# A graph-network kernel: the ratios of its multi-head attention stage as outer products of key and query rows

## The chip, the cores and the metric

One core of one Trainium2 chip runs the whole kernel. The metric is device time in microseconds of one execution; less is better.

## The reference

64 graphs with 128 nodes of 256 features go through two layers. Layer 0 is softmax attention with 8 heads over masked logits, then a feed-forward block. Layer 1 is graph attention twice: first with 8 heads, then with one. What the change touches is the first of these, for each head:

```python
s = jnp.einsum('bhnk,hk->bhn', h, a_src)
t = jnp.einsum('bhnk,hk->bhn', h, a_dst)
e = jax.nn.leaky_relu(s[:, :, :, None] + t[:, :, None, :], ALPHA)   # ALPHA = 0.2
e = e + bias[:, None, :, :]
attn = jax.nn.softmax(e, axis=-1)
out = jnp.einsum('bhij,bhjk->bhik', attn, h)
```

`bias` is the adjacency matrix, the same for all heads. Since exp(leaky_relu(z)) is the larger of exp(z) and exp(0.2 z), an unnormalised weight is exp(bias) times factors of the row and of the column times max(exp(0.8 (s + t)), 1). The part with max is a rank-one ratio compared with 1.

## The kernel before

The work runs in four stages, A (layer-0 attention), B (feed-forward), C (8-head graph attention) and D (one head). Each goes over the 64 graphs in 16 chunks of four graphs (512 nodes, `W4`). Every engine has its own hand-written instruction list; semaphores join them, and each engine runs strictly in the order that its list gives. Steps 2 to 13 of a stage are a loop of two steps (`chunks`).

Stage C, the subject here, is software-pipelined over two chunks: step i does the front of chunk i and the back of chunk i-1.

The front, in order of data: ScalarE normalises chunk i (`normalise`, `xn`, L944, done at the end of the step before). TensorE transposes it to the PSUM tiles F0 and F1 (`ln_turn`, L1130). ScalarE copies it out as `xh` (L898), VectorE subtracts to get the low part `xl` (`ln_lo`, L293). TensorE then transposes the adjacency into F0 (`adj_turn`, L1184) and computes the score rows s and t of all heads into F1 (`c_st`, L1105 to L1107, six matmuls). VectorE takes row maxima (`rows_max`, `tmx`, L526), ScalarE turns them into shifts (`rows_shift`, `tms`, L1049 and L1050) and exponentiates the rows (`rows_exp`, `rb`, L1056), VectorE caps them (`rows_cap`, L530), TensorE transposes them (`c_b_turn`, L1345), and ScalarE copies them out as rounded rows `rp` (L1024) and columns `bqs` (L1063, with L1064). GpSimd adds the low part of the rows (`rows_lo`, L854). TensorE computes the value rows with `tall` (L1121 to L1123, 24 matmuls in a step), and VectorE scales them into `hb` (`hb_out`, L534).

The back, for each of the 8 heads of chunk i-1: TensorE broadcasts a row of `rp` over all partitions with a selection matmul (`c_bcast`, L1373, 512 columns), VectorE builds the weights `pp` in four instructions of 128 columns, one for each graph, because the column's factor is a scalar of that graph (`c_scale`, L575), and TensorE multiplies by the values in four column tiles (`c_av`, L1385, 16 matmuls in the program, 32 in the trace). The heads alternate between two PSUM banks and two `pp` buffers, so they run one after another:

```python
pe.matmul(BK[:, h % 2, :], sel[:, h, :], rp[par][:], start=True, stop=True).then_inc(c_bc, 1)
...
r = dve.scalar_tensor_tensor(out=pp[h % 2][:, g, :], in0=BK[:, h % 2, g * P:(g + 1) * P],
                             scalar=bq_sb[par][:, g, 16 + h:17 + h], in1=gts(i, g),
                             op0=ALU.max, op1=ALU.mult)
```

At the end ScalarE copies the outputs (`c_out_copy`, `o_sb`, L1083, four copies), VectorE takes reciprocals (`c_recip`, L583) and GpSimd adds the result to x (`residual`, L862 and L868). VectorE also takes the statistics of the next chunk (L276, L281).

## Time and profile before

| | us |
|---|---|
| median of 3 runs (1198.71 to 1200.44) | 1198.84 |
| the profiled execution, its own time | 1199.37 |
| its span in the profile | 1196.3 |
| busy in the span: TensorE, VectorE, ScalarE, GpSimd | 1122.2, 831.5, 704.1, 448.9 |
| busy from 840 to 1035 us (inside stage C) | TensorE 177.38, VectorE 190.25, ScalarE 105.77, GpSimd 147.91 of 195.00 |

Stage C runs from about 814 us (the adjacency transpose of its first chunk) to about 1050 us (its last output copy). Busy time counts an engine from the start of an instruction to its end; successive instructions of an engine overlap a little, so a pitch (start to start) is shorter than a duration. The shares over the whole span mix four stages; the last line of the table is the one that speaks of stage C.

### The profile page before, as it was taken

To read this page: it belongs to the slowest core of one execution; us is meant where nothing else is said; L and a number is where in the kernel's file an instruction comes from. 1 tells how busy PE (TensorE), PEld (TensorE's weight loads), DVE (VectorE), ACT (ScalarE), POOL (GpSimd) and SP (SyncE) were. 2 spreads that over 40 slices of the span, in tenths; PEclk is the share of its full clock that TensorE was granted. 3 is DMA by queue.
4 is the path that set the end of the run, shared out by engine and by line. 5 is a ranking of instruction groups with operands and counts; after the bars stand their busy time and mean duration, and the time that the engine had idled before them with its cause. 6 is when DMAs were issued, how large, how long until landed. Compare 5 with 4: busy or idle time off the path is not lost.

```text
span 1196.3 us, 39899 instructions
## 1 busy us (share of the span) xinstructions
PE 1122.2 (94%) x15260; PEld 966.6 (81%) x15260; DVE 831.5 (70%) x2259; ACT 704.1 (59%) x1734; POOL 448.9 (38%) x657
## 2 busy tenths in 40 slices
PE   5699999999999989999999999998999999869998
PEld 5588888888888769989998998896767667658886
DVE  5676777677777764455445544546999999958886
ACT  2467776777677763355345434543555555559996
POOL 2531212121212112123112311213777777867764
PEclk9799999999999999999999999999999999979999
DMA  8021020111000000000000000000000000002212
GB/s 227 2 73 29 28 55 28 28 29 55 28 12 11 11 2 1 1 1 0 0 0 0 0 0 0 0 1 19 21 18 18 18 18 18 4 1 71 70 53 88
DMA packets 41733, 31.13 MB, mean 26 GB/s; under 512 B 5280, under 2 KB 41376, under 8 KB 41632
## 3 DMA queue, kind: packets, MB, share of 16 engines
q1 hardware_dynamic: 36736, 28.84, 7.8%
q10 hardware_dynamic: 4896, 0.80, 0.6%
q8 instruction: 80, 1.31, 0.4%
q14 instruction: 21, 0.17, 0.1%
HBM read 21.25 MB, written 8.39 MB: 25 GB/s over the span
## 4 chain that ended last, share of the span: by engine, by line
PE 77%; DVE 11%; issue 4%; ACT 4%; POOL 2%; DVEq 1%; DMA 1%; SPq 0%; ACTq 0%; POOLq 0%
PE BK L1229 6%; PE BK L1105 5%; PE BK L1106 5%; PE BK L1107 5%; PE BK L1315 5%; PE BK L1313 5%; PE BK L1314 5%; DVE pp L575 4%; PE BK L1203 4%; PE BK L1215 4%; PE F L1105 3%; PE BK L1196 3%; PE F L1107 3%; PE F L1106 3%; PE F L1130 3%
## 5 line engine op out<-in xcount | busy, mean ns | idle before, releaser
L1005 ACT ACTIVATE gf<-BK,bcol 128x512 f32<-128x512 f32 x128 | 88.3, 690 | 190.6 <-PE BK L1107 176.9
L806 POOL TENSOR_TENSOR ve<-mv,eps_l 128x4 f32<-128x4 f32 x64 | 15.7, 245 | 458.7 <-DVE mv L281 458.7
L924 ACT ACTIVATE e_sb<-BK,nmx 128x128 f32<-128x128 f32 x512 | 141.7, 402 | 28.5 <-DVE nmx L413 28.5
L1313 PE MATMUL BK<-wf_hi,gh 128*128 128x256 f32 x512 | 146.0, 285 | 0.0
L1315 PE MATMUL BK<-wf_lo,gh 128*128 128x256 f32 x512 | 144.8, 283 | 0.0
L1314 PE MATMUL BK<-wf_hi,gl 128*128 128x256 f32 x512 | 143.5, 280 | 0.0
L575 DVE SCALAR_TENSOR_TENSOR pp<-BK,bqs,gt_all 128x128 f32<-128x128 f32 x512 | 137.6, 336 | 3.3 <-PE BK L1385 2.5
L506 DVE TENSOR_TENSOR gl<-gf,gh 128x512 fp32r<-128x512 f32 x128 | 91.7, 716 | 69.1 <-ACT gh L1006 67.0
L419 DVE TENSOR_TENSOR pt_sb<-BK,ft 128x512 f32<-128x512 f32 x128 | 85.1, 686 | 69.2 <-PE BK L1203 67.5
L520 DVE TENSOR_TENSOR x_all<-BK,x_all 128x256 f32 (+1 forms) x64 | 27.2, 425 | 127.4 <-PE BK L1315 127.4
L944 ACT ACTIVATE xn<-x_all,neg_mr,rstd 128x256 f32 (+1 forms) x188 | 100.1, 604 | 24.5 <-POOL neg_mr L815 24.4
L276 DVE BATCH_NORM_STATS2 st<-x_all 128x6 f32 (+1 forms) x256 | 96.8, 413 | 7.7 <-DMA x_all<-in_x_dram 7.6
L1105 PE MATMUL BK<-xh,wf_hi 128*128 128x512 f32 x256 | 101.6, 397 | 0.5 <-DVE x_all L435 0.5
L1106 PE MATMUL BK<-xl,wf_hi 128*128 128x512 f32 x256 | 101.5, 396 | 0.0
L1107 PE MATMUL BK<-xh,wf_lo 128*128 128x512 f32 x256 | 101.4, 396 | 0.0
L1314 PEld LDWEIGHTS BK<-wf_hi,gl 128*128 128x128 f32 x512 | 97.4, 190 | 0.0
L1313 PEld LDWEIGHTS BK<-wf_hi,gh 128*128 128x128 f32 x512 | 96.1, 188 | 0.0
L1315 PEld LDWEIGHTS BK<-wf_lo,gh 128*128 128x128 f32 x512 | 95.8, 187 | 0.0
L783 POOL TENSOR_TENSOR x_all<-x_all,c_bc 128x256 f32 (+1 forms) x128 | 90.0, 737 | 8.6 <-POOL rp L854 8.1
L413 DVE TENSOR_REDUCE nmx<-BK 128x8 f32<-128x1024 f32 x64 | 76.7, 1219 | 23.3 <-PE BK L1196 23.3
L783 POOL TENSOR_TENSOR x_all<-x_all,bo_bc 128x256 f32 (+1 forms) x64 | 44.9, 737 | 125.3 <-ACT xn L944 125.3
L1006 ACT ACTIVATE gh<-BK,bcol 128x512 fp32r<-128x512 f32 x128 | 87.2, 681 | 0.0
(193 smaller groups left out, 2996.8 us busy)
## 6 DMA issues: line engine op xcount, KB each, us to landing
x_all<-in_x_dram SPq DMA_DIRECT2D x16, 512.0 KB, 4.3
adj_in<-in_adj_dram SPq DMA_DIRECT2D x32, 256.0 KB, 2.8
out_dram<-y SPq DMA_DIRECT2D x16, 512.0 KB, 2.9
s_wf<-in_L_gnn_Wf_dram SPq DMA_DIRECT2D x2, 1024.0 KB, 11.8
s_w<-in_L_gnn_W_dram SPq DMA_DIRECT2D x2, 256.0 KB, 7.6
s_wq<-in_L_gnn_Wq_dram SPq DMA_DIRECT2D x1, 256.0 KB, 3.6
s_wk<-in_L_gnn_Wk_dram SPq DMA_DIRECT2D x1, 256.0 KB, 4.1
s_wv<-in_L_gnn_Wv_dram SPq DMA_DIRECT2D x1, 256.0 KB, 4.9
```

The costliest lines, as they stand in the source:

```text
L276: dve.bn_stats(st[:, g, :], xs(i, g)).then_inc(ln_st, 1)
L506: dve.tensor_tensor(gl[:, f, :], gf[f % 2][:], gh[:, f, :].bitcast(F32), ALU.subtract).then_inc(b_gl, 1)
L575: r = dve.scalar_tensor_tensor(out=pp[h % 2][:, g, :], in0=BK[:, h % 2, g * P:(g + 1) * P], scalar=bq_sb[par][:, g, 16 + h:17 + h], in1=gt ...
L783: pool.tensor_tensor(xs(i, g), xs(i, g), bias[:], ALU.add).then_inc(signal, 1)
L924: e = act.activation(e_sb[:, j, :], LE[:, r, q, :], ACT.Exp, bias=nmx[:, j:j + 1], scale=1.0)
L944: act.activation(xn[:, g, :], xs(nxt, g), ACT.Identity, scale=rstd[:, g:g + 1], bias=neg_mr[:, g:g + 1]).then_inc(ln_xn, 1)
L1105: pe.matmul(dst, w_hi, m_hi, start=start, stop=False)
L1106: pe.matmul(dst, w_hi, m_lo, start=False, stop=False)
L1107: return pe.matmul(dst, w_lo, m_hi, start=False, stop=stop)
L1313: pe.matmul(dst, gh[:, f, n], hi[:, f, :], start=(f == 0), stop=False)
L1314: pe.matmul(dst, gl[:, f, n], hi[:, f, :], start=False, stop=False)
L1315: r = pe.matmul(dst, gh[:, f, n], lo[:, f, :], start=False, stop=(f == FT - 1))
```

## The change

In stage C alone, the row broadcast goes. The score rows of four heads now lie in four groups of 32 partitions, key rows and query rows in one tile. VectorE takes minima (`row_minima`), ScalarE moves them to the other half of the partitions (`far_minima`, two tiny activations), VectorE combines them (`row_shifts`), ScalarE exponentiates (`row_exps`: four activations with a scale and a bias that are both columns in memory), VectorE caps (`row_limits`). ScalarE then makes two tiles `inv` with the halves exchanged (`inverse_rows`, two activations of 64 partitions x 512 columns for each group of four heads). `ratios` computes exp(0.8 (s + t)) as outer products: 16 matmuls for four heads, in four row tiles of the array, into four banks. VectorE needs no column factor any more, the constant 1 takes its place, so `c_scale` is one instruction of 512 columns for a head. Two banks are left for outputs; heads are collected in groups of 3, 3 and 2, each copied out by one activation. There are four `pp` buffers and two `o_sb` buffers. `rows_lo` and the copy to `rp` leave stage C. Stage D keeps its own path with a smaller `sel`. The setup computes masks and scales for the new layout, in place of the wide `sel`: 17 more small VectorE instructions (11 for masks by partition, 5 more for the weights of the rows, 1 for their bias).

The order within a step is rewritten on all engines. The core of the diff:

```diff
+HEAD_GROUPS = ((0, 3), (3, 3), (6, 2))
...
-        sel = sb("sel", [P, H, P], F32R)
+        sel = sb("sel", [P, P], F32R)
...
+        o_sb = [o(f"o_sb{r}", [P, G, H * HA]) for r in range(2)]
-        pp = [o(f"pp{r}", [P, G, P]) for r in range(2)]
-        o_sb = o("o_sb", [P, G, H * HA])
+        pp = [o(f"pp{r}", [P, G, P]) for r in range(4)]
+        row_e = o("row_e", [P, W4])
+        row_c = o("row_c", [P, W4])
+        inv = [o(f"inv{r}", [P, W4]) for r in range(2)]
...
-                done(dve.tensor_tensor(sel[:], ident[:, 0:H].unsqueeze(2).to_broadcast([P, H, P]),
-                                       ident[:, 32:32 + H].unsqueeze(2).to_broadcast([P, H, P]), ALU.add))
+                done(dve.tensor_tensor(sel[:], ident[:, 0:1].to_broadcast([P, P]), ident[:, 32:33].to_broadcast([P, P]), ALU.add))
...
+            def row_minima(i):
+                dve.wait_ge(c_st_done, i + 1)
+                dve.tensor_reduce(row_mn[:], ROW[CC][:].rearrange("p (g n) -> p g n", n=P), AX, ALU.min).then_inc(r_mn, 1)
+            def row_shifts(i):
+                dve.wait_ge(r_far, i + 1)
+                dve.wait_ge(r_mn, i + 1)
+                dve.scalar_tensor_tensor(out=row_sh[:], in0=row_mn[:], scalar=own_row[:, 0:1], in1=far_mx[:],
+                                         op0=ALU.mult, op1=ALU.add).then_inc(r_sh, 1)
+            def row_limits(i):
+                dve.wait_ge(r_e, i + 1)
+                wait_for(dve, r_q, i * 2)
+                dve.tensor_scalar(row_c[:], row_e[:], row_cap[:, 0:1], None, ALU.min).then_inc(r_c, 1)
             def hb_out(e, par, n):
...
-            def c_scale(i, par, h):
-                dve.wait_ge(c_bc, i * H + h + 1)
+            def c_scale(i, h):
+                dve.wait_ge(r_q, i * 2 + h // 4 + 1)
                 dve.wait_ge(c_gt, i + 1)
-                wait_for(dve, c_o, i * H + (h - 1))
-                for g in range(G):
-                    r = dve.scalar_tensor_tensor(out=pp[h % 2][:, g, :], in0=BK[:, h % 2, g * P:(g + 1) * P],
-                                                 scalar=bq_sb[par][:, g, 16 + h:17 + h], in1=gts(i, g),
-                                                 op0=ALU.max, op1=ALU.mult)
-                r.then_inc(c_pp, 1)
...
             def c1_step(i, half, par):
                 back = not (isinstance(i, int) and i == 0)
-                for h in range(H):
-                    if back:
-                        c_scale(i - 1, 1 - par, h)
-                    c1_front(i, par, h)
-                    if h == 1 and back and not (isinstance(i, int) and i == 1):
-                        c_recip(i - 2)
+                if back:
+                    c_scale(i - 1, 0)
+                if back and not (isinstance(i, int) and i == 1):
+                    c_recip(i - 2, par)
+                if back:
+                    c_scale(i - 1, 1)
+                    ln_lo(i + CC)
+                    c_scale(i - 1, 2)
+                    c_scale(i - 1, 3)
+                row_minima(i)
+                next_stats(i, (0, 1))
+                row_shifts(i)
+                next_stats(i, (2, 3))
+                dve.wait_ge(ln_st, (i + CC + 2) * G)
+                if back:
+                    c_scale(i - 1, 4)
+                aggr(i + CC + 1)
+                row_limits(i)
+                if back:
+                    c_scale(i - 1, 5)
+                    c_scale(i - 1, 6)
+                    c_scale(i - 1, 7)
+                dve.wait_ge(c_bq, i + 1)
+                hb_out(i, par, 0)
+                hb_out(i, par, 1)
...
+                        add_bias(i, CC, c1_bc, c_xb)
+                        if not (isinstance(i, int) and i < 2):
+                            residual_share(i - 2, par)
-                        rows_lo(i, par)
-                        add_bias(i, CC, c1_bc, c_xb)
+                    if first == CC and not (isinstance(i, int) and i < 2):
+                        residual_sum(i - 2)
...
+            def c1_step(i, half, par):
+                back = not (isinstance(i, int) and i == 0)
+                if back and not (isinstance(i, int) and i == 1):
+                    c_out_copy(i - 2, par, 2)
+                if back:
+                    ln_hi(i + CC)
+                act.wait_ge(adj_t, i + NC + 1)
+                act.activation(gt_all[:, bass.ds(i * W4, W4)], F[0][:], ACT.Exp).then_inc(c_gt, 1)
+                if back:
+                    c_out_copy(i - 1, 1 - par, 0)
+                far_minima(i)
+                row_exps(i)
+                inverse_rows(i, 0)
+                bq_out(i, par, 0)
+                if back:
+                    c_out_copy(i - 1, 1 - par, 1)
+                normalise(i, CC, range(G))
+                inverse_rows(i, 1)
+            def far_minima(i):
+                act.wait_ge(r_mn, i + 1)
+                wait_for(act, r_sh, i)
+                for to, of in ((0, 64), (64, 0)):
+                    r = act.activation(far_mx[to:to + 64, :], row_mn[of:of + 64, :], ACT.Identity, bias=cb[0][of:of + 64, 0:1],
+                                       scale=far_row[of:of + 64, 0:1])
+                r.then_inc(r_far, 1)
+            def row_exps(i):
+                act.wait_ge(r_sh, i + 1)
+                wait_for(act, r_c, i)
+                for g in range(G):
+                    r = act.activation(row_e[:, g * P:(g + 1) * P], ROW[CC][:, g * P:(g + 1) * P], ACT.Exp, bias=row_sh[:, g:g + 1],
+                                       scale=row_sign[:, 0:1])
+                r.then_inc(r_e, 1)
+            def inverse_rows(i, t):
+                act.wait_ge(r_c, i + 1)
+                for to, of in ((0, 64), (64, 0)):
+                    r = act.activation(inv[t][to:to + 64, :], row_c[of:of + 64, :], ACT.Copy, scale=half_row[of:of + 64, t:t + 1])
+                r.then_inc(r_inv, 1)
...
+            def c_out_copy(i, par, k):
+                first, heads = HEAD_GROUPS[k]
+                if k == 0:
+                    wait_for(act, c_att, (i - 1) * G + C_START)
+                act.wait_ge(c_o, i * H + first + heads)
+                act.activation(o_sb[par][:, :, first * HA:(first + heads) * HA],
+                               BK[:, 4 + (par + k) % 2, 0:G * heads * HA].rearrange("p (g c) -> p g c", g=G), ACT.Copy).then_inc(c_ev, 1)
...
-            def c_bcast(i, par, h):
-                pe.wait_ge(c_rp, i + 1)
-                pe.wait_ge(c_lo, i + 1)
-                wait_for(pe, c_pp, i * H + (h - 1))
-                pe.matmul(BK[:, h % 2, :], sel[:, h, :], rp[par][:], start=True, stop=True).then_inc(c_bc, 1)
+            def ratios(i, t):
+                pe.wait_ge(r_inv, i * 2 + t + 1)
+                pe.wait_ge(c_one, i + 1)
+                wait_for(pe, c_pp, i * H + 4 * t)
+                for g in range(G):
+                    n = slice(g * P, (g + 1) * P)
+                    for r in range(4):
+                        rows = slice(r * 32, r * 32 + 4)
+                        m = pe.matmul(BK[:, r, n], inv[t][rows, n], row_c[rows, n], start=True, stop=True, tile_position=(r * 32, 0))
+                m.then_inc(r_q, 1)
...
+            def c_h_out(g):
+                r = tall(F[g // 2][:, (g % 2) * D:(g % 2 + 1) * D], "w1", g, g % 2 == 0)
+                if g % 2 == 1:
+                    r.then_inc(c_h, 1)
             def c1_step(i, half, par):
                 back = not (isinstance(i, int) and i == 0)
-                for h in range(H):
-                    if back and h < H - 1:
-                        c_bcast(i - 1, 1 - par, h + 1)
-                    c1_front(i, half, par, h)
-                    if h == H - 2:
-                        c_bcast(i, par, 0)
-                    if back:
-                        c_av(i - 1, 1 - par, h)
+                if back:
+                    ratios(i - 1, 0)
+                c_turn(i, CC)
+                if back:
+                    c_av(i - 1, 1 - par, 0)
+                adj_turn(i + CC, half, par, CC)
+                if back:
+                    c_av(i - 1, 1 - par, 1)
+                c_st(i, CC, 0)
+                c_st(i, CC, 1)
+                if back:
+                    c_av(i - 1, 1 - par, 2)
+                    c_av(i - 1, 1 - par, 3)
+                    ratios(i - 1, 1)
+                pe.wait_ge(c_gt, i + 1)
+                c_h_out(0)
+                c_h_out(1)
+                if back:
+                    c_av(i - 1, 1 - par, 4)
+                row_turn(i)
+                pe.wait_ge(r_e, i + 1)
+                c_h_out(2)
+                c_h_out(3)
+                if back:
+                    c_av(i - 1, 1 - par, 5)
+                    c_av(i - 1, 1 - par, 6)
+                    c_av(i - 1, 1 - par, 7)
...
```

What the order looks like on TensorE around the transpose of the exponentiated rows, in a loop step of before (`rb` are the rows, `sel` the broadcast, `hb,pp` a head's output):

```order
L1385 MATMUL BK<-hb_95,pp_103 32x33 [waits c_pp]
L1385 MATMUL BK<-hb_95,pp_103 32x33 x15
L1373 MATMUL BK<-rp_99,sel 128x512 [waits c_pp,c_lo,c_rp]
L1345 MATMUL F<-ident,rb 128x128 [waits c_rb]
L1345 MATMUL F<-ident,rb 128x128 x3
L1376 REGISTER_ALU
L1385 MATMUL BK<-hb_95,pp_104 32x33 [waits c_pp]
```

and in a loop step of the change (`row_c` are the capped rows; L1212 is the first of the 12 value matmuls of two graphs, L1470 a head's output):

```order
L1470 MATMUL BK<-hb_100,pp_108 32x33 [waits c_pp]
L1470 MATMUL BK<-hb_100,pp_108 32x33 x15
L55 ISA [waits r_c]
L1437 MATMUL BK<-ident,row_c 128x128 [waits c_pp]
L1437 MATMUL BK<-ident,row_c 128x128 x3
L1212 MATMUL F<-w_hi,xh 128x256 [waits r_e]
```

Before, outputs of three heads still follow the transpose one by one with their broadcasts between them. In the change, 12 value matmuls stand behind the transpose, and the outputs of heads 5, 6 and 7 stand behind those.

On ScalarE, in a loop step of the change, from the exponentials to the end of the step (`o_sb` is the copy of heads 3 to 5 of the chunk before, `xn` the normalisation of the next chunk):

```order
L1105 ACTIVATE row_e<-F,row_sh,row_sign 128x128 [waits r_c,r_sh]
L1105 ACTIVATE row_e<-F,row_sh,row_sign 128x128 x3
L1112 ACTIVATE inv_117<-row_c,half_row 64x512 [waits r_c]
L1112 ACTIVATE inv_117<-row_c,half_row 64x512
L1152 ACTIVATE bqs_101<-BK 128x4x8 [waits r_t]
L1155 ACTIVATE hb_99<-BK 128x32
L1174 REGISTER_ALU
L1175 ACTIVATE o_sb_98<-BK 128x4x99 [waits c_o]
L1003 ISA [waits ln_nm]
L1005 ISA [waits ln_t]
L1005 ACTIVATE xn<-x_all,neg_mr,rstd 128x256
```

Before, the normalisation follows directly on the two small copies of the transposed rows, and all output copies stand at the start of a step. Now a copy that waits for head 5 stands ahead of the normalisation.

## Rows read from the trace of the kernel before

**Rows 1.** Windows: us, busy PE, PEld, DVE, ACT, POOL, granted clock, DMA share, GB/s

```profile
840.00:1035.00 195.00, 177.38 (x4189) 136.54 (x4187) 190.25 (x641) 105.77 (x271) 147.91 (x230) 1.00 0.06 17
...
822.00:825.00 3.00, 3.00 (x14) 2.35 (x14) 0.97 (x3) 1.48 (x4) 2.92 (x5) 0.51 0.00 0
...
1045.00:1050.00 5.00, 3.03 (x131) 1.79 (x131) 3.61 (x14) 0.74 (x3) 1.54 (x3) 1.00 0.02 3
```

**Rows 2.** Groups by line of VectorE, 840 to 1035: xcount | busy us, mean ns | idle

```profile
L575 DVE SCALAR_TENSOR_TENSOR pp<-BK,bqs,gt_all 128x128 f32<-128x128 f32 x433 | 116.4, 335 | 3.0 <-PE BK L1385 2.5
L293 DVE TENSOR_TENSOR xl<-F,xh 128x512 fp32r<-128x512 f32 x28 | 17.9, 681 | 0.0
...
L530 DVE TENSOR_SCALAR rb<-rb 40x512 f32<-40x512 f32 x14 | 10.3, 738 | 0.0
L526 DVE TENSOR_REDUCE tmx<-F 24x4 f32<-24x512 f32 x14 | 9.7, 692 | 1.7
...
L583 DVE RECIPROCAL crec<-o_sb 128x32 f32<-128x32 f32 x14 | 4.7, 335 | 0.0
```

**Rows 3.** Timeline of ScalarE, 900 to 930: start us, us, [idle before]

```profile
903.15 0.39 ACT L1049 ACTIVATE tms<-tmx,cb,msc 24x4 f32<-24x4 f32 x1 [2.52 <-DVE tmx L526]
...
917.51 0.39 ACT L1049 ACTIVATE tms<-tmx,cb,msc 24x4 f32<-24x4 f32 x1 [2.52 <-DVE tmx L526]
...
918.39 1.12 ACT L1056 ACTIVATE rb<-F,tms 40x128 f32<-40x128 f32 x4
...
922.56 2.08 ACT L944 ACTIVATE xn<-x_all,neg_mr,rstd 128x256 f32 x4 [0.32 <-POOL neg_mr L815]
925.29 1.24 ACT L1083 ACTIVATE o_sb<-BK 128x264 f32<-128x264 f32 x4 [0.65 <-PE BK L1385]
```

**Rows 4.** Groups by line, whole span: VectorE and ScalarE forms near the new ones

```profile
L419 DVE TENSOR_TENSOR pt_sb<-BK,ft 128x512 f32<-128x512 f32 x128 | 85.1, 686 | 69.2 <-PE BK L1203 67.5
...
L1072 ACT ACTIVATE hb<-BK,bqs 128x256 f32<-128x256 f32 x64 | 26.9, 472 | 5.7 <-PE BK L1123 4.2 <-issue 0.3
...
L930 ACT ACTIVATE att_t<-BK 128x256 f32<-128x256 f32 x64 | 25.5, 399 | 36.8 <-PE BK L1222 36.8
...
L1024 ACT ACTIVATE rp<-rb 40x512 fp32r<-40x512 f32 x16 | 10.1, 632 | 17.0 <-DVE rb L530 17.0
...
L354 DVE TENSOR_TENSOR sel<-ident 128x1024 fp32r<-128x1024 f32 x1 | 1.2, 1207 | 0.0
```

**Rows 5.** Timeline of TensorE in stage C: start us, us

```profile
814.41 0.48 PE L1105 MATMUL F<-xh,wst_hi 128*128 128x512 f32 x1
...
815.66 0.40 PE L1107 MATMUL F<-xh,wst_lo 128*128 128x512 f32 x1
...
913.60 0.66 PE L1184 MATMUL F<-ident,adj_in 128*128 128x128 f32 x4 [0.33 <-DVE xl L293]
...
916.61 0.46 PE L1385 MATMUL BK<-hb,pp 128*32 128x33 f32 x32
917.00 0.50 PE L1373 MATMUL BK<-rp,sel 128*128 128x512 f32 x1
917.33 0.28 PE L1121 MATMUL F<-w_hi,xh 128*128 128x256 f32 x1
...
921.23 0.60 PE L1345 MATMUL F<-ident,rb 128*128 128x128 f32 x4
...
922.49 0.28 PE L1121 MATMUL F<-w_hi,xh 128*128 128x256 f32 x1
...
924.04 0.49 PE L1373 MATMUL BK<-rp,sel 128*128 128x512 f32 x1
```

**Rows 6.** Timeline of TensorE in stage A: 16 f32 matmuls in four row tiles

```profile
301.50 1.17 PE L1196 MATMUL BK<-k,q 32*128 32x128 f32 x32
302.60 0.76 PE L1215 MATMUL BK<-v,pt_sb 128*32 128x33 f32 x64
```

**Rows 7.** Tile rb in stage D: duration ns min/median/max, first and last start

```profile
L530 DVE TENSOR_SCALAR rb<-rb x15: 410/419/707, 1059.9 to 1177.7; 40x512 f32<-40x512 f32 x15
```

More of the change, by code:

```diff
@@ L43 @@
 ROWS = 40
+HEAD_GROUPS = ((0, 3), (3, 3), (6, 2))
+FACTOR_SHIFT = 40.0
+RATIO_LIMIT = 5.5e34
+FACTOR_LIMIT = 6.4e17
 TROW = 96
@@ new lines, in inverse_rows, with c2_front @@
+            def inverse_rows(i, t):
[3 more added lines that the diff above has]
+                r.then_inc(r_inv, 1)
+            def c2_front(i, par):
+                if not (isinstance(i, int) and i == 0):
+                    d_hb(i - 1, 1 - par, 1)
+                normalise(i, CD, range(G))
+                rows_shift(i)
+                wait_for(act, c_lo, i)
+                rows_exp(i)
+                if not (isinstance(i, int) and i == NC - 1):
+                    d_hi(i + 1, 1 - par)
+                wait_for(act, d_bc, i - 1)
+                act.wait_ge(c_rb, i + 1)
+                act.activation(rp[par][0:ROWS, :], rb[0:ROWS, :], ACT.Copy).then_inc(c_rp, 1)
+                bq_out(i, par, 1)
@@ L1077, in _ @@
             act.wait_ge(c_zero, 6)
-            def c_out_copy(i):
-                wait_for(act, c_att, i * G + C_START)
-                for g in range(G):
-                    act.wait_ge(c_o, (i + 1) * H)
-                    act.activation(o_sb[:, g, :], BK[:, 2 + g, 0:H * HA], ACT.Copy).then_inc(c_ev, 1)
-            def c1_step(i, half, par):
-                if not (isinstance(i, int) and i < 2):
-                    c_out_copy(i - 2)
-                c_front(i, par, CC)
+            def c_out_copy(i, par, k):
[5 more added lines that the diff above has]
+                               BK[:, 4 + (par + k) % 2, 0:G * heads * HA].rearrange("p (g c) -> p g c", g=G), ACT.Copy).then_inc(c_ev, 1)
             chunks(act, c1_step)
-            c_out_copy(NC - 2)
+            last = (NC - 1) % 2
+            c_out_copy(NC - 2, 1 - last, 2)
             d_hi(0, 0)
-            c_out_copy(NC - 1)
+            for k in range(len(HEAD_GROUPS)):
+                c_out_copy(NC - 1, last, k)
             def c2_step(i, half, par):
-                c_front(i, par, CD)
+                c2_front(i, par)
                 d_hb(i, par, 0)
@@ L1375, in c_av @@
             def c_av(i, par, h):
+                k = h // 3
+                first, heads = HEAD_GROUPS[k]
                 pe.wait_ge(c_pp, i * H + h + 1)
@@ L1403, in _ @@
             last = (NC - 1) % 2
-            for h in range(H):
-                if h < H - 1:
-                    c_bcast(NC - 1, last, h + 1)
-                c_av(NC - 1, last, h)
+            for t in range(2):
+                ratios(NC - 1, t)
+                for h in range(4 * t, 4 * t + 4):
+                    c_av(NC - 1, last, h)
             def d_bcast(i, par):
-                pe.wait_ge(c_rp, i + NC + 1)
-                pe.wait_ge(c_lo, i + NC + 1)
+                pe.wait_ge(c_rp, i + 1)
+                pe.wait_ge(c_lo, i + 1)
                 wait_for(pe, d_pp, i * G)
-                pe.matmul(BK[:, 0, :], sel[:, 0, :], rp[par][:], start=True, stop=True).then_inc(d_bc, 1)
+                pe.matmul(BK[:, 0, :], sel[:], rp[par][:], start=True, stop=True).then_inc(d_bc, 1)
             def d_av(i, par, g):
```

223 lines of the change are left out of this document (107 added, 116 removed).

## The prediction

> **What bounds the kernel now.** The change touches stage C and a little of the setup, so I read the windows first, and of them the one that lies inside stage C [rows 1]. VectorE is busy 190.25 of 195.00 us there, 97.6%, against 91% of TensorE, 54% of ScalarE and 76% of GpSimd. The timeline of ScalarE gives the length of a step: the same shift instruction starts at 903.15 and at 917.51 [rows 3], 14.36 us a chunk. The groups of VectorE [rows 2] say what fills it: L575, the weights, takes 116.4 us; 433 instructions are 13.5 chunks of 32, so 8.6 us of each 14.36. The rest of VectorE's work is 14.0 - 8.6 = 5.4 us a chunk. So VectorE's throughput bounds stage C, and more than half of it is what the change rewrites.
>
> TensorE's timeline [rows 5] gives pitches (start to start). A head's output takes 0.39 (916.61 to 917.00), a broadcast 0.34 (917.00 to 917.33), 12 value matmuls 1.55 (922.49 to 924.04), four transposes at most 0.60, the six score matmuls 1.25 from first to last start. In a chunk: 8 x 0.39 + 8 x 0.34 + 24 value matmuls 3.1 + 1.5 for the scores + 16 transposes 2.2 = 12.6 us.
>
> **The change, throughput first.** VectorE: 32 instructions of 128 columns become 8 of 512. The nearest row reads PSUM and memory over 512 columns in 0.686 [rows 4]; successive ones overlap by about 0.08, so 0.60 each, 4.8 instead of 8.6. Maxima to minima is the same instruction; the cap goes from 40 to 128 partitions at 512 columns, same length. The new `row_shifts` has 4 columns: under the 0.335 of the 32-column reciprocal [rows 2] and over nothing, I take 0.17. VectorE would need 10.4 us.
> TensorE: 8 broadcasts (2.7) go, two groups of 16 f32 matmuls in four row tiles come. Stage A has this form with 32 rows a tile instead of 4: 1.10 from start to the next start [rows 6]. The columns that stream are the same, so 2.2: 12.1 us.
> ScalarE: 7.8 us a chunk now; minus the copy to `rp` (0.63), plus four inverse copies (below) 2.5, plus 0.4 for the exponentials: 10.1. GpSimd loses `rows_lo`.
> No engine is above 12.1 us. If throughput decided, a chunk would fall by some 2 us. It doesn't say what the waits do, so I followed the chain that returns to itself after one step.
>
> **The loop of waits in the new order.** It starts where normalisation starts on ScalarE.
> 1. Four `xn`: 2.08 less an overlap of 0.10, 1.98 [rows 3].
> 2. Behind them in the queue, the second pair of inverse copies. A copy of 512 columns from memory takes 0.632, and a scale that is a column in memory adds 0.07 (472 ns for 256 columns against 399) [rows 4]: 0.70 each, 1.20 to the next start.
> 3. The last output copy (264 columns) 0.40, the reciprocal on VectorE that waits for it 0.26 to the next start, then `pp` of head 1, 0.60. Only now comes `ln_lo`: 0.68 for its first half [rows 2]. The transposes and `xh` are ready earlier.
> 4. TensorE: adjacency 0.60, head 1 0.39, scores 1.65 (814.41 to the end of the last, 815.66 + 0.40) [rows 5].
> 5. Minima 0.69 [rows 2]; two small activations, 0.39 each [rows 3], 0.79; `row_shifts` 0.17.
> 6. Four exponentials. Before, with a bias column, four took 1.12 [rows 3], 0.356 the last and 0.255 apart. Now the scale is a column too. I add 0.1 to each: 1.54. Lower end 1.12; upper end the four `xn` with both columns, 2.08.
> 7. The cap. 0.738 in stage C, 0.419 in stage D [rows 2, 7]. In stage C GpSimd was adding tensors at that moment; in the new order its only work then is the tiny `ve`. I take 0.42, and 0.74 is the upper end.
> 8. TensorE: transposes of the rows 0.55, 12 value matmuls 1.51, head 5 0.46 [rows 5]. These follow strictly, although head 5 needs neither.
> 9. ScalarE: the copy of heads 3 to 5, 0.40 to the next start, which stands ahead of the normalisation in the queue: back at 1.
>
> The sum is 14.29. Nine hand-overs between engines lie in it; from the shifts' end to the exponentials' start there are 0.09 us (917.51 + 2 x 0.39 to 918.39) [rows 3], I take 0.06 each, 0.55. The loop branch, once in two steps, and register work between waits: 0.15. So 15.0 us a step, against 14.36 now. TensorE stands idle almost 3 us of it: about 1.7 for `ln_lo` (its first half is done 3.1 after the `xn` end: 1.20 + 0.40 + 0.26 + 0.60 + 0.68 less 0.10, with hand-overs; eight transposes and head 0 fill 1.4), the rest before the transposes of `xn` and of the rows. The freed 3.8 us of VectorE are waits, hidden behind the loop.
>
> The ScalarE steps are where a rule of the skill can be weighed. Four exponentials with one column operand took 1.12 us [rows 3]. The Trainium skill, "ScalarE: Activation LUTs", section "What ACT_TABLE_LOAD costs", puts an activation at 186 ns plus 0.833 ns an element plus about 93 ns for each pointer operand, with about 93 ns of overlap. By that the old four would take 1.27, so it is high for a PSUM source, and the new four 1.64; the sum would be 15.1 instead of 15.0.
>
> **Sum.** 14 steps run at full length with both halves: 14 x 0.64 = +9.0 us. Draining the last chunk: before 8 heads at 4 x 0.27 (116.4 / 433) behind a broadcast, about 9.0; after, two `ratios` with hand-over at 1.2, 8 x 0.60 and an output, 7.5: -1.5. Setup, on VectorE's list before stage A is in swing: `sel` (1.207) [rows 4] shrinks to an eighth, -1.0; 17 small instructions come, each under 0.335 [rows 2]; at 0.12, +2.0; net +1.0, with 0 and +3 as ends. Total +8.5. The profiled execution took 1199.37, 0.53 over the median: 1207.9, and **1207** against the median of 1198.84.
>
> **Rivals.**
> *Throughput decides (faster).* The loop falls apart if one long link is not in it: above all if head 5 ends before the normalisation's inputs are ready, or if `ln_lo` doesn't wait for the last output copy. Then a step is TensorE's 12.1 plus about 1 us of waits, 13.1: 14 x -1.26 = -17.6, with drain and setup -18, 1180. The point is where the loop passes under 14.36: 0.64 shorter than I sum it. Low exponentials (-0.42) and inverse copies at 0.6 (-0.2) bring it only just there. For it speaks that VectorE has 4 us to spare; against it, that both waits stand ahead of their followers in a strict queue. 0.15.
> *Nothing gained.* The low ends of 6 and 2 together: 14.4, and 1199. 0.13.
> *Slower than the sum: the TensorE clock.* TensorE would be idle 3 of 15 us, now 1.3. In rows 1 the granted clock is 0.51 from 822 to 825, at 1.2 GHz, after TensorE had been mostly waiting for the first chunk's rows; it is 1.00, 2.4 GHz, from 1045 to 1050 with 3.03 of 5 us busy. If the clock fell in the 1.7 us gap, scores, adjacency and outputs behind it would double: about +2 us a step, 17.0, 1236. The second row has TensorE idler than the new order would, so 0.06. The Trainium skill, "TensorE: Matmul & The Clock Gate", Part 1, says that the gate follows how busy the engine has been, which would give 1236 by the same working; by that rule alone I would give it more.
> *The change doesn't do what it says:* row tiles that run one after another would make `ratios` 4.4 us; 2 x 3.3 less TensorE's slack beside them (1.2) is 5.4 a step, 1283; rows 6 show the form at 1.10. Under 0.01.
> My own case, the loop at 14.7 to 15.4 (exponentials 0.3 shorter, or the cap at 0.74), holds 0.65: 1202 to 1217.
>
> **How the numbers follow.** About 0.2% (2.4 us) is what a measurement of this kernel can tell from no change. Faster 0.15 is the first rival, same 0.13 the second, slower 0.72 my case with the clock and the fourth. The range reaches from 1188, which takes in half of the throughput case, to 1220, with the upper ends of the links; outside are about 0.08 below and 0.10 above.
>
> **What would show it.** In the profile after: `pp` with 128x512, x128, near 0.68 us each; VectorE busy in stage C down from 97.6% to about 70%, ScalarE up to about 68%; a step of 15.0 us from one `far_mx` to the next; `ratios` 1.1 us from start to the next start; a wait of ScalarE at `o_sb` for TensorE's output in each step of about 1 us, and TensorE waiting more than 1 us for `xl` before the adjacency. I am wrong if a step is under 14.4 us, if ScalarE's normalisation waits for GpSimd's `neg_mr` instead of following `o_sb`, or if stage C, 236 us from 814 to 1050 now, doesn't become 7 to 10 us longer.

## The result, and the profile after

The changed kernel takes 1227.3 us (median of 4 runs, 1226.1 to 1227.97) against 1198.9 before (1198.71 to 1200.44): the ratio is 1.0232, interval 1.0219 to 1.0245. It is slower, as forecast, but by 28 us instead of 8, and above the range. The profiled execution took 1226.1 us with a span of 1224.3.

The page of the changed kernel: span, busy time of TensorE and VectorE, the granted clock in 40 slices, and the group of scaling copies (busy us, mean ns | idle before).

```profile
span 1224.3 us, 41293 instructions
...
PE 1127.3 (92%) x16156; PEld 984.7 (80%) x16156; DVE 781.3 (64%) x1908; ACT 743.7 (61%) x1766; POOL 426.7 (35%) x641
...
PEclk9799999999999999999999999998778877779999
...
L614 DVE SCALAR_TENSOR_TENSOR pp<-BK,gt_all 128x512 f32<-128x512 f32 x128 | 82.5, 678 | 34.3 <-PE BK L1454 31.8
```

The copies are what was foreseen, 8 a chunk of 0.678 us where there were 32 of 0.335 us [rows 2], and VectorE has 50 us less to do (781.3 against 831.5). But nine slices of the clock row, from 826 us to 1102, nearly all of stage C and the first of stage D, stand at 7 and 8. The windows of the changed kernel (columns as in [rows 1]: us, busy PE, PEld, DVE, ACT, POOL, granted clock), first most of stage C, then one step of it in pieces of 2 us:

```profile
860.00:1030.00 170.00, 145.09 (x3657) 120.57 (x3656) 106.58 (x240) 103.21 (x220) 95.83 (x160) 0.80 0.05 15
...
888.00:890.00 2.00, 1.88 (x16) 1.84 (x16) 1.96 (x4) 1.77 (x4) 1.50 (x5) 1.00 0.00 0
890.00:892.00 2.00, 1.57 (x110) 1.38 (x112) 1.12 (x2) 1.38 (x3) 2.00 (x3) 1.00 0.00 0
892.00:894.00 2.00, 1.65 (x34) 1.46 (x30) 0.69 (x1) 1.96 (x5) 1.48 (x4) 0.85 0.00 0
894.00:896.00 2.00, 1.49 (x37) 1.01 (x35) 0.89 (x3) 1.93 (x4) 2.00 (x4) 0.50 0.00 0
896.00:898.00 2.00, 1.34 (x24) 1.01 (x28) 2.00 (x5) 0.09 (x1) 2.00 (x5) 0.50 0.00 0
898.00:900.00 2.00, 2.00 (x32) 1.65 (x24) 0.40 (x1) 0.51 (x1) 0.37 (x1) 0.50 0.29 86
900.00:902.00 2.00, 2.00 (x83) 1.50 (x86) 1.12 (x3) 0.66 (x2) 0.00 (x0) 0.94 0.15 45
```

The granted clock that was 1.00 from 840 to 1035 us [rows 1] is now 0.80 on average: once in every step it falls from 2.4 to 1.2 GHz and comes back. With two levels, a mean of 0.80 means that it is at half for 0.4 of each step, 6.8 of 17.04 us. VectorE is busy 63% (106.58 of 170). What the half clock does is in the timeline of the changed kernel, one step (start us, duration us):

```profile
884.80 0.78 ACT L1097 ACTIVATE far_mx<-row_mn,cb,far_row 64x4 f32<-64x4 f32 x2
...
890.62 0.51 ACT L1175 ACTIVATE o_sb<-BK 128x396 f32<-128x396 f32 x1 [0.79 <-PE BK L1470]
891.02 2.06 ACT L1005 ACTIVATE xn<-x_all,neg_mr,rstd 128x256 f32 x4
...
893.14 1.75 PE L1221 MATMUL F<-ident,xn 128*128 128x128 f32 x8 [0.35 <-ACT xn L1005]
894.58 0.39 ACT L1175 ACTIVATE o_sb<-BK 128x264 f32<-128x264 f32 x1
...
896.66 1.12 PE L1275 MATMUL F<-ident,adj_in 128*128 128x128 f32 x4 [1.18 <-DVE xl L312]
...
897.71 0.67 PE L1470 MATMUL BK<-hb,pp 128*32 128x33 f32 x32
...
898.31 0.80 PE L1196 MATMUL F<-xh,wst_hi 128*128 128x512 f32 x1
...
900.88 0.69 DVE L581 TENSOR_REDUCE row_mn<-F 128x4 f32<-128x512 f32 x1 [2.48 <-PE F L1198]
...
901.84 0.38 ACT L1097 ACTIVATE far_mx<-row_mn,cb,far_row 64x4 f32<-64x4 f32 x1
```

A step is 17.04 us (884.80 to 901.84), against 14.36 [rows 3]. The waits of the changed kernel in 825 to 1050 (us in total, times, longest) are those that the loop was built from: ScalarE's output copies for TensorE, and TensorE for `xl`.

```profile
ACT o_sb L1175 <- PE BK L1470: 47.1, 26, 3.1
...
DVE crec L620 <- ACT o_sb L1175: 23.3, 14, 2.0
...
PE F L1275 <- DVE xl L312: 15.6, 13, 2.0
```

Something else moved that the change doesn't touch. Stage B, whose code is the same, runs from 444.9 to 797.8 us instead of 447.4 to 813.2: 352.9 us long instead of 365.8. The tile view of its matmuls (ns min/median/max, first and last start), before:

```profile
L1313 PE MATMUL BK<-wf_hi,gh x512: 279/286/365, 447.4 to 813.0; 128*128 128x256 f32 x171
...
L1315 PE MATMUL BK<-wf_lo,gh x512: 276/281/285, 447.8 to 813.2; 128*128 128x256 f32 x171
```

and after:

```profile
L1404 PE MATMUL BK<-wf_hi,gh x512: 276/276/369, 444.9 to 797.6; 128*128 128x256 f32 x171
...
L1406 PE MATMUL BK<-wf_lo,gh x512: 276/276/281, 445.3 to 797.8; 128*128 128x256 f32 x171
```

So the 28.0 us between the spans are: -2.5 up to stage B, -12.9 in it, +39.5 in the 15 steps of stage C (first to last row minima 253.6 us; before, first to last shift 214.1), and +3.9 between stage B and these steps and behind them.

### The profile page after: what moved, and what is told of

It is laid out like the page before. It is cut to its first block, busy times and chain, and to the rows that moved or that the text cites. A ratio compares the mean times of both kernels' runs of the same rounds, so it can differ in the third digit from the quotient of the medians.

```text
span 1224.3 us, 41293 instructions
## 1 busy us (share of the span) xinstructions
PE 1127.3 (92%) x16156; PEld 984.7 (80%) x16156; DVE 781.3 (64%) x1908; ACT 743.7 (61%) x1766; POOL 426.7 (35%) x641
## 4 chain that ended last, share of the span: by engine, by line
PE 71%; ACT 9%; DVE 8%; issue 6%; POOL 3%; ACTq 1%; DVEq 1%; DMA 0%; POOLq 0%
PE BK L1320 5%; PE BK L1198 5%; PE BK L1197 5%; PE BK L1196 5%; PE BK L1404 5%; PE BK L1405 5%; PE BK L1406 5%; PE BK L1294 4%; PE F L1196 4%; PE BK L1306 4%; PE F L1221 3%; PE F L1197 3%; PE F L1198 3%; PE BK L1287 3%; ACT xn L1005 2%
## 5 line engine op out<-in xcount | busy, mean ns | idle before, releaser
L862 POOL TENSOR_TENSOR ve<-mv,eps_l 128x4 f32<-128x4 f32 x64 | 15.1, 236 | 533.0 <-DVE mv L300 533.0
L1404 PE MATMUL BK<-wf_hi,gh 128*128 128x256 f32 x512 | 142.9, 279 | 0.0
L1406 PE MATMUL BK<-wf_lo,gh 128*128 128x256 f32 x512 | 141.5, 276 | 0.0
L614 DVE SCALAR_TENSOR_TENSOR pp<-BK,gt_all 128x512 f32<-128x512 f32 x128 | 82.5, 678 | 34.3 <-PE BK L1454 31.8
L1221 PE MATMUL F<-ident,xn 128*128 128x128 f32 x512 | 78.4, 304 | 13.9 <-ACT xn L1005 13.6
```

The costliest lines, as they stand in the source:

```text
L1221: r = pe.transpose(F[kt][:, g * P:(g + 1) * P], xn[:, g, kt * P:(kt + 1) * P], ident[:])
L1404: pe.matmul(dst, gh[:, f, n], hi[:, f, :], start=(f == 0), stop=False)
L1406: r = pe.matmul(dst, gh[:, f, n], lo[:, f, :], start=False, stop=(f == FT - 1))
```

## The experiments

There were two questions: where stage C lost 39 us, and why stage B is shorter. For the first my theory was the loop of waits with the falling clock on top of it; the rivals were that the loop is longer than summed, whatever the clock, or that TensorE is bound by its own work. For the second the theory was the place of tiles in memory: `sel` shrinks by 3584 bytes a partition and small tiles are new, so that the tiles behind them move by 3424 bytes. Among them is what stage B multiplies: `gh` starts at byte 163904 of a partition instead of 167328, and `xh` and `xl` at the same place as `gh` modulo 256. The weights lie ahead of `sel` and don't move. The rival was something carried over from stage A.

### Stage B: tiles moved, nothing else

The kernel before with an unused tile ahead of those that moved:

```diff
         exp_bias = sb("exp_bias", [P, 1])
+        sb("pad", [P, 8])
```

> The kernel before with 32 bytes of unused memory ahead of the activation tiles, so that xh, xl, gh and gl start at a multiple of 64 bytes, as they do in the changed kernel (before: 32 over a multiple of 64). Theory (the start address sets the pitch of stage B's matmuls, 0.120 us against 0.116 for 256 columns): stage B 13 us shorter, stage C unchanged at 236.6, about 1186 us. Rival (stage B got faster for another reason, such as the code's place or the run): 1199 us, pitch 0.120.

Measured: 1192.89 us (1191.27 to 1193.68), ratio 0.9949 (0.9933 to 0.9966). Stage B took 446.4 to 806.3, 359.9 us. The place counts, but half of the effect was missing. The same pad in the changed kernel:

> The changed kernel with the same 32 bytes, which puts its activation tiles 32 over a multiple of 64. Theory of the start address: stage B takes 366 us again, 1240 us. Rival: no change, 1227 us.

Measured: 1239.73 us (1237.26 to 1240.03), stage B 363.3 us (447.3 to 810.6). Moving 32 bytes takes the gain away again, so it belongs neither to the changed code nor to stage A. Larger pads in the kernel before (`[P, 168]`, `[P, 40]` and `[P, 104]`) ask which distance counts:

> The kernel before with an unused tile of 672 bytes a partition ahead of the tiles of stage B, so that they start at the same place within 4096 bytes as in the changed kernel (32 bytes gave 1192.9 us, stage B 360 us long instead of 366; the changed kernel's is 353). If the start within a larger stride than 64 bytes decides, stage B is about 353 us and the time about 1186 us. If only the start within 64 bytes counts, it is 1193 us as with 32 bytes, and the other 7 us of the changed kernel's stage B come from the order of the tiles among themselves.

> The kernel before with an unused tile of 160 bytes a partition: the tiles of stage B then start at the same place within 512 bytes as with 672 bytes (1184.0 us), but not within 1024, 2048 or 4096. If the place within 512 bytes or less decides, stage B is 353 us long and the time about 1184 us; if a larger stride counts, it stays between that and the 1192.9 us that 32 bytes gave, or above.

> The kernel before with an unused tile of 416 bytes a partition: the tiles of stage B start at the same place within 256 bytes as with 160 and 672 bytes (1183.3 and 1184.0 us), but 256 bytes off within 512. If the place within 256 bytes or less decides, stage B is 353 us long again and the time 1182 to 1185 us; if it is the place within 512, stage B is longer and the time above 1187 us.

Measured: 1183.97 us (1182.44 to 1185.85), 1183.32 (1182.1 to 1184.34) and 1183.47 (1182.1 to 1184.44), the last with ratio 0.9868 (0.9852 to 0.9885). The tile view of the kernel before with 416 bytes:

```profile
L1314 PE MATMUL BK<-wf_hi,gh x512: 276/276/369, 445.9 to 797.9; 128*128 128x256 f32 x171
...
L1316 PE MATMUL BK<-wf_lo,gh x512: 276/276/278, 446.2 to 798.2; 128*128 128x256 f32 x171
```

By the start byte of `gh`:

| kernel | start mod 256 | mod 512 | stage B, us |
|---|---|---|---|
| before | 160 | 416 | 365.8 |
| changed, 32 bytes on | 96 | 96 | 363.3 |
| before, 32 bytes on | 192 | 448 | 359.9 |
| before, 672 bytes on | 64 | 64 | 352.9 |
| before, 160 bytes on | 64 | 64 | 352.8 |
| before, 416 bytes on | 64 | 320 | 352.3 |
| changed | 64 | 64 | 352.9 |

The four with 64 agree within 0.6 us, whatever the place within 512. So stage B's -12.9 us is a gift of memory placement. Part of the -2.5 us ahead of stage B is too: with the pads of 160, 416 and 672 bytes stage B begins at 445.5, 445.9 and 445.8 us instead of 447.4. The fair partner of the changed kernel is the moved kernel before with 1184.0 us, and against it the change costs 43 us, not 28. Which of the moved tiles makes the difference, and through what, was not tried.

### Stage C: work that nobody reads

The clock fell where TensorE had waits in every step. If the fall is part of the price, filling a wait buys it back:

```diff
+                if back:
+                    for n in range(7):
+                        pe.matmul(BK[:, 4 + (1 - par) % 2, 396:512], ident[:], ident[:, 0:116], start=True, stop=True)
                 adj_turn(i + CC, half, par, CC)
```

> The changed kernel with seven f32 matmuls of 116 columns into unused columns of a bank, in each step between the output of head 0 and the adjacency transposes, where TensorE waits for xl. They fill about 1.35 us of the wait at full clock. Theory (of the 17.05 us of a step, 15.0 are the loop of waits and 2.0 the fallen clock): the clock stays at 1.0, a step takes 15.0 to 15.3, total about 1199 us. Rival (the loop alone is 17 us long, and the clock only falls because TensorE waits): the step stays at 17 or grows by up to 1.4, 1227 to 1248 us.

Measured: 1212.62 us (1209.8 to 1215.71), 14.7 us under the changed kernel, with 7 matmuls a step more. The timeline of this kernel, one step in which the clock stayed at 1.00 (L1489 are the filler matmuls; each stands in the trace as two):

```profile
880.73 1.50 ACT L1105 ACTIVATE row_e<-F,row_sh,row_sign 128x128 f32<-128x128 f32 x4 [0.29 <-DVE row_sh L586]
...
882.37 0.48 DVE L592 TENSOR_SCALAR row_c<-row_e,row_cap 128x512 f32<-128x512 f32 x1
...
882.98 0.65 PE L1437 MATMUL BK<-ident,row_c 128*128 128x128 f32 x4 [0.30 <-DVE row_c L592]
883.39 0.37 PE L1212 MATMUL F<-w_hi,xh 128*128 128x256 f32 x1
...
884.94 1.06 PE L1470 MATMUL BK<-hb,pp 128*32 128x33 f32 x96
885.48 0.51 ACT L1175 ACTIVATE o_sb<-BK 128x396 f32<-128x396 f32 x1 [0.79 <-PE BK L1470]
885.88 2.06 ACT L1005 ACTIVATE xn<-x_all,neg_mr,rstd 128x256 f32 x4
...
887.96 1.45 ACT L1112 ACTIVATE inv<-row_c,half_row 64x512 f32<-64x512 f32 x2
...
889.40 1.82 PE L1489 MATMUL BK<-ident 128*128 128x116 f32 x14
889.44 0.39 ACT L1175 ACTIVATE o_sb<-BK 128x264 f32<-128x264 f32 x1
...
891.51 0.66 PE L1275 MATMUL F<-ident,adj_in 128*128 128x128 f32 x4 [0.29 <-DVE xl L312]
...
892.49 0.50 PE L1196 MATMUL F<-xh,wst_hi 128*128 128x512 f32 x1
...
894.18 0.69 DVE L581 TENSOR_REDUCE row_mn<-F 128x4 f32<-128x512 f32 x1 [0.93 <-PE F L1198]
...
895.14 0.78 ACT L1097 ACTIVATE far_mx<-row_mn,cb,far_row 64x4 f32<-64x4 f32 x2
...
896.21 1.50 ACT L1105 ACTIVATE row_e<-F,row_sh,row_sign 128x128 f32<-128x128 f32 x4 [0.29 <-DVE row_sh L586]
```

It separates the two causes, because this step and that of the changed kernel are the same up to the adjacency transposes: from `far_mx` to there 11.86 us in both (884.80 to 896.66; 879.65 to 891.51). Behind them the half clock adds, to the head 0.46 (1.05 against 0.59), to the scores 0.21 (0.60 against 0.39), to the minima 0.88 (2.57 against 1.69), together 1.55. The loop by itself is 15.48 us (880.73 to 896.21), and with the clock 17.04. The transposes of `xn`, 1.75 instead of 1.09, cost nothing: `xl` is waited for anyway.

In five of its 15 steps the clock still fell (16.5 to 16.7 us each, where the others from the third step on took 15.5 to 15.7), so the fill was a partial cure. That is some 5 us of the 13.6 over the 1199 expected; 7 more are the loop, 15.5 instead of 15.0. In such a step the fillers themselves ran at half clock:

```profile
905.09 3.34 PE L1489 MATMUL BK<-ident 128*128 128x116 f32 x14
...
908.22 0.66 PE L1275 MATMUL F<-ident,adj_in 128*128 128x128 f32 x4
```

They took 3.34 us instead of 1.82, more than the gap holds, and pushed the adjacency transposes back: no wait for `xl` is left ahead of them. Four of these matmuls instead of seven:

> The changed kernel with four instead of seven matmuls of 116 columns that nobody reads ahead of the adjacency transposes: about 1.05 us of work in a gap of about 2.1 us (with seven it was 1.82 us, and 0.3 us of the gap was left). A step in which the clock held took 15.49 us there, one in which it fell 17.05. If what decides is that TensorE isn't left idle in this gap, four hold the clock in fewer steps than seven: between 1213 and 1227 us. If any work in the gap is enough, the time is that with seven or less, 1206 to 1213 us.

Measured: 1206.23 us (1205.08 to 1207.94). The time is that of the second theory, but it isn't a proof of it, because the clock did not hold more often. In the profiled executions it fell in 7 of 15 steps with four fillers (0.95 in 860 to 1030 us) and in 5 of 15 with seven (0.97). What is less is the price of a fall: 15.8 to 16.3 us for such a step instead of 16.5 to 16.7. Four fillers just about fit into the gap even at half clock:

```profile
904.36 2.04 PE L1489 MATMUL BK<-ident 128*128 128x116 f32 x8
```

Less fill was faster, then, not better at holding the clock. The steps account for 2.4 of the 4.9 us between the two profiled executions; 1.0 was there before stage B began, and the rest lies behind the steps and isn't explained. One execution of each is profiled, so that 7 and 5 may be chance. That 1206 is so near the forecast's 1207 is luck: the 15 steps are 19.8 us longer than before where 9.0 was forecast, and the placement, which the forecast didn't have, takes 12.9 off.

### Stage C: one link out of the loop

ScalarE's copy of heads 3 to 5 stood ahead of the normalisation. Behind it:

```diff
-                if back:
-                    c_out_copy(i - 1, 1 - par, 1)
                 normalise(i, CC, range(G))
+                if back:
+                    c_out_copy(i - 1, 1 - par, 1)
                 inverse_rows(i, 1)
```

> The changed kernel with ScalarE's copy of heads 3 to 5 behind the normalisation instead of ahead of it. Theory of the loop: the wait for head 5 leaves the loop, and the step is 0.8 us shorter at whatever clock: 14.4 with the clock full (1190 us), 16.2 with the clock falling once a step (1214 us); I expect the second. Rival (the copy was not on the path): no change, 1227 us.

Measured: 1220.64 us (1219.03 to 1222.96), 6.7 us less than the changed kernel where 13 was expected. From its fourth step to its 14th a step took 17.0 to 17.2 us as in the changed kernel; the first three and the last were shorter, together by 3.4 us. The timeline of TensorE in this kernel says why:

```profile
895.00 1.11 PE L1275 MATMUL F<-ident,adj_in 128*128 128x128 f32 x4 [1.52 <-DVE xl L312]
...
896.64 0.80 PE L1196 MATMUL F<-xh,wst_hi 128*128 128x512 f32 x1
...
898.94 0.63 PE L1198 MATMUL F<-xh,wst_lo 128*128 128x512 f32 x1
899.50 1.11 PE L1470 MATMUL BK<-hb,pp 128*32 128x33 f32 x64
900.54 1.38 PE L1454 MATMUL BK<-row_c,inv 4*128 4x128 f32 x32
```

All six scores, and the outputs and ratios behind them, now run at half clock; in the changed kernel the last scores and what follows are fast again (900.77 0.78). The fall begins later behind the row minima (11.5 us against 9.5) and covers more of what the loop waits for: the clock took back what the link gave. With four filler matmuls as well:

> Four of these matmuls, and ScalarE's copy of heads 3 to 5 behind the normalisation. If the normalisation is what the step waits for, it starts 0.8 us or more sooner, and the time is 11 us or more under that with the four matmuls alone. If the chain beside it (ratios of the last two heads, their scaling copy, their value matmuls, the last output copy) ends at the same time, as the copy alone let one think with 6.6 us of gain, it is 3 to 7 us under it.

Measured: 1193.84 us (1191.92 to 1197.95), 12.4 under the four matmuls alone, ratio 0.9962 (0.9947 to 0.9977). With the clock mostly held (0.99 in 860 to 1030) the same edit is worth twice as much, and the mean step is 14.84 instead of 15.59. Not all of it is the link: from the third on, steps at full clock went from 15.5 to 15.6 down to 14.9 to 15.1, and the clock fell in 2 steps instead of 7. The copy was a link of the loop, as summed, and edits on such a loop can only be priced together with the clock.

### Stage C: the links out of the loop

The reciprocal moves on VectorE, the last output copy, the second pair of inverse copies and the copy of heads 3 to 5 on ScalarE:

```diff
                     c_scale(i - 1, 0)
-                if back and not (isinstance(i, int) and i == 1):
-                    c_recip(i - 2, par)
...
                 row_minima(i)
+                if back and not (isinstance(i, int) and i == 1):
+                    c_recip(i - 2, par)
...
-                if back and not (isinstance(i, int) and i == 1):
-                    c_out_copy(i - 2, par, 2)
                 if back:
                     ln_hi(i + CC)
+                if back and not (isinstance(i, int) and i == 1):
+                    c_out_copy(i - 2, par, 2)
...
                 if back:
+                    inverse_rows(i - 1, 1)
                     c_out_copy(i - 1, 1 - par, 0)
...
+                normalise(i, CC, range(G))
                 if back:
                     c_out_copy(i - 1, 1 - par, 1)
-                normalise(i, CC, range(G))
-                inverse_rows(i, 1)
...
+            inverse_rows(NC - 1, 1)
```

> The changed kernel with its links taken out of the loop: on ScalarE the copies of the last output and of heads 3 to 5 and the inverse copies are issued behind what the next step waits for, and on VectorE the reciprocal of the last group goes behind the row minima. No arithmetic is changed. Loop of waits with the clock on top (my theory): the step is then near VectorE's and TensorE's own work, about 13.2 us where the changed kernel takes 17.05, TensorE's granted clock stays above 0.97 in 860 to 1030 us, and the time is 1227 - 14 x 3.9 = about 1173 us (1165 to 1185). Rival, TensorE is bound by its own work at whatever clock it gets: the clock stays near 0.80 and the time above 1215 us. Rival, another wait of the same size takes the place of each: 1195 to 1215 us.

Measured: 1178.71 us (1178.56 to 1181.83), ratio 0.9834 (0.9815 to 0.9853). It beats the changed kernel by 48.6 us and the kernel before by 20. Of those 20 some 15 are the placement of stage B: against the moved kernel before (1183.97, run on the same chip) the gain is 5.3 us, and the two sets of runs do not overlap. A step takes 13.89 us on average (first to last row minima, 801.93 to 1010.27, 15 steps), more than the 13.2 that I expected. The window of this kernel:

```profile
860.00:1030.00 170.00, 147.62 (x4498) 124.97 (x4498) 128.49 (x283) 122.91 (x259) 116.08 (x192) 0.97 0.05 15
```

TensorE is busy 147.62 of 170, 12.06 us a step, at a clock of 0.97; VectorE 10.5. One step in which the clock fell took 15.68, the others 12.5 to 14.25. So the "throughput" numbers of the forecast, 12.1 and 10.4, were right, and about 1.8 us of waits remain, where the rival "throughput decides" had 1. The same with the narrow copies:

```diff
-                dve.scalar_tensor_tensor(out=pp[h % 4][:].rearrange("p g n -> p (g n)"), in0=BK[:, h % 4, :], scalar=1.0,
-                                         in1=gt_all[:, bass.ds(i * W4, W4)], op0=ALU.max, op1=ALU.mult).then_inc(c_pp, 1)
+                for g in range(G):
+                    r = dve.scalar_tensor_tensor(out=pp[h % 4][:, g, :], in0=BK[:, h % 4, g * P:(g + 1) * P], scalar=1.0,
+                                                 in1=gts(i, g), op0=ALU.max, op1=ALU.mult)
+                r.then_inc(c_pp, 1)
```

> As the kernel with the links cut, but with each 512-column scaling copy on VectorE done as four of 128 columns, as before the change (the constant 1 stays). It prices the wide copies where VectorE bounds: 8 copies of 0.68 us against 32 of about 0.22 is +1.6 us a step if VectorE bounds, so 14.8 us a step and about 1195 us. If TensorE or a loop of waits bounds instead, the difference is under 0.5 us a step and the time within 7 us of the other.

Measured: 1197.03 us (1194.0 to 1201.65), as the first theory said, but by another way. Its windows:

```profile
860.00:1030.00 170.00, 144.57 (x4136) 121.47 (x4136) 138.75 (x537) 117.54 (x250) 108.50 (x180) 0.96 0.06 16
```

VectorE is busy 82%, not bound. Undisturbed steps take 14.4 us, 0.2 to 0.6 more than with wide copies; but in six of the 15 the clock falls and they take 16.2 to 16.3 (it falls in the first step too, which takes 14.1). So of the 18.3 us some 11 (6 x 1.8) are again the clock. And four filler matmuls on the kernel with the links cut:

> As the kernel with the links cut, with four matmuls of 116 columns that nobody reads ahead of the four adjacency transposes, where TensorE was idle. If the clock still falls with the links cut, this gives back what it costs and the time is under that kernel's by 5 us or more; if it stays up already, the filler is hidden in idle time or costs at most 4 x 0.1 us a step, 0 to +6 us.

Measured: 1184.66 us (1183.72 to 1190.47), 6.0 more: 4 x 0.1 us in each of 15 steps. The clock fell in one step, as without them. Where the clock holds, filler is plain cost.

## Why the prediction was wrong

The lengths of a step, worked out from the starts of the row minima (before: of the shifts), beside the steps in which the granted clock of the profiled execution fell, and its mean in 860 to 1030 us:

| kernel | mean step, us | clock fell in, of 15 | clock | time, us |
|---|---|---|---|---|
| before | 14.27 | 1 | 1.00 | 1198.9 |
| changed | 16.91 | 15 | 0.80 | 1227.3 |
| copy late | 16.66 | 15 | 0.80 | 1220.6 |
| 7 fillers | 15.75 | 5 | 0.97 | 1212.6 |
| 4 fillers | 15.59 | 7 | 0.95 | 1206.2 |
| 4 fillers, copy late | 14.84 | 2 | 0.99 | 1193.8 |
| links cut, narrow copies | 15.05 | 7 | 0.96 | 1197.0 |
| links cut, 4 fillers | 14.28 | 1 | 0.99 | 1184.7 |
| links cut | 13.89 | 1 | 0.97 | 1178.7 |

**What bounds before, and the throughput after: right.** VectorE's 10.4 us a step was measured as 10.7 in the changed kernel (106.58 / 170 x 17.04), ScalarE's 10.1 as 10.3, the ratios' 1.10 start to start as 1.11 (884.43 to 885.54), TensorE's 12.1 as 12.06 in the kernel with the links cut, where the clock mostly held.

**The loop of waits: right in its links, 0.5 us short.** At full clock the loop is 15.48 us against 15.0. Each link read from the filler kernel's timeline, hand-overs included, beside the forecast's 14.29 without them:

| link | forecast | measured | from |
|---|---|---|---|
| 1 four `xn` | 1.98 | 2.08 | 885.88 to 887.96 |
| 2 inverse copies | 1.20 | 1.48 | to 889.44 |
| 3 copy, reciprocal, head 1, `xl` | 1.94 | 2.07 | to 891.51 |
| 4 adjacency, head 1, scores | 2.64 | 2.67 | to 894.18 |
| 5 minima, far, shifts | 1.65 | 2.03 | to 896.21 |
| 6 four exponentials | 1.54 | 1.64 | 880.73 to 882.37 |
| 7 cap | 0.42 | 0.61 | to 882.98 |
| 8 transposes, values, head 5 | 2.52 | 2.50 | to 885.48 |
| 9 copy of heads 3 to 5 | 0.40 | 0.40 | to 885.88 |
| sum | 14.29 | 15.48 | |

Two terms were small: the second inverse copy doesn't overlap the first (1.45 for two of 0.72, and 0.03 behind them, where I took 1.20), and links 5 and 7 hold more than their busy time (together 0.57 over the forecast where 0.06 a hand-over was set; 0.11 of it are a longer cap, 0.48 against 0.42, and a longer `row_shifts`, 0.22 against 0.17). The exponentials, with the widest bounds, were good: 1.50 busy against 1.54. The Trainium skill, "ScalarE: Activation LUTs", section "What ACT_TABLE_LOAD costs", would have given an estimate of 1.64, a tenth too much for this form. 0.48 x 14 = 6.7 us of the miss are the longer loop.

**The clock: the step that failed.** The rival had the mechanism, the place (adjacency, head and scores behind the `xl` gap) and almost the price (2 us a step; 1.55 over the real loop), and got 0.06, because [rows 1] shows 1.00 from 1045 to 1050 with TensorE busy 3.03 of 5 us. That one stretch was taken as a proof that short waits don't lower the clock, and the term stood at nothing in the sum. It wasn't comparable: it says nothing of what the engine did before it or of a pattern that comes back in every step. Nor was the window behind it read, in the same trace:

```profile
1050.00:1052.00 2.00, 0.00 (x0) 0.00 (x0) 1.47 (x4) 0.49 (x2) 0.00 (x0) 0.69 0.00 0
```

There the clock falls in the kernel before as well, from 1.00 in 1050 to 1050.5 us to 0.50 in 1051 to 1051.5; TensorE's last output had started at 1048.66. In the changed kernel the fall comes in 892 to 894 us, behind stretches that were 1.88 and 1.57 of 2 us busy, so busier than that row. The price was 14 x 1.56 = 21.8 us where the sum had 0. The Trainium skill, "TensorE: Matmul & The Clock Gate", Part 1, told the direction, and its section "A second HAM failure mode: psum-queue depth-cycling" tells of another kernel in which TensorE was idle briefly and often between groups of matmuls and the clock went back and forth between its two levels. This case's trace shows the same (in the step shown the longest idle time is 1.18 us, in the others at most 2.0). A rule that spoke against the change was outvoted by one row.

**The placement: not seen at all.** -12.9 us in stage B, from tiles that the diff moves. Without it the time would have been about 1240 (the changed kernel with 32 bytes took 1239.7), near the clock rival's own 1236.

**Sum.** The forecast had +9.0 for the steps; it was +39.5 over 15 of them, of which 14 full ones hold 14 x 1.12 = 15.7 for the loop and 21.8 for the clock. Setup and stage A came out at -2.5 where +1.0 stood (of this 1.5 to 1.9 the pads alone gave), and what lies between and behind the steps at +3.9 where -1.5 stood: the drain isn't shorter but longer, 22.1 us from the last minima (1054.39) to the end of the last output copy (1076.53) against 19.1 from the last maxima before (1031.38 to 1050.50), with the granted clock at 0.50 from 1065 to 1080.

**The rivals.** "Throughput decides" is nearest to what the kernel with the links cut does, and it needed just the edits that take the links out. That it took 1178.7 where 1180 was priced is luck: its steps are 13.89 us instead of 13.1, some 12 us over 15 of them, and the placement of stage B gives 12.9 back. The row tiles ran side by side (1.11).

## What to carry to other kernels

When a freed engine turns a throughput bound into a loop of waits, sum the loop link by link, but price TensorE's new idle time as a risk of half clock in the work behind it, unless a row shows the same pattern repeated at full clock; then take the links that needn't be there out of the loop before judging the arithmetic, here 48.6 us by order alone. Compare a change that adds or shrinks tiles with a version of the old kernel whose tiles start at the same place modulo 256 bytes, or an effect of placement (here 15 of 1199 us, 1.3%) is credited to the change. And read a filler's price at half clock too: seven matmuls that fit into the gap at full clock did not fit at half.

## What the runs showed of the hardware

Not expected: the start of the tiles in a partition changes the pace of stage B's matmuls. A start of `gh` at 64 modulo 256 gave 352.3 to 352.9 us in four layouts, 192 gave 359.9, 96 363.3 and 160 365.8, with the same instructions, TensorE busy throughout and the clock at 1.00.

Also not expected: how near two patterns can lie of which one keeps the clock. From 884 to 920 us TensorE is busy 31.08 of 36 us in the changed kernel, where the clock falls in each step, and in the kernel with the links cut 31.31 of 36, where it stays at 1.00. The first of the two holds work stretched by the half clock, so its share at full clock would be lower, and the pieces just ahead of a fall say more: 1.88 and 1.57 of 2 us busy in the changed kernel, and here two in the kernel with the links cut that are no busier, without a fall behind them:

```profile
902.00:904.00 2.00, 1.70 (x22) 1.64 (x15) 2.00 (x4) 1.70 (x4) 1.71 (x4) 1.00 0.00 0
904.00:906.00 2.00, 1.57 (x104) 1.33 (x106) 1.31 (x3) 1.81 (x5) 1.79 (x3) 1.00 0.00 0
```

What in the pattern decides was not settled by these runs.
